# Second product of the quarter behind: two places of two slot tiles each instead of four places of one

## The reference, cut to what matters

```
h   = einsum('bsd,bdh->bsh', x, W[cat]) + b[cat]        # 4096 x 512
probs = softmax(h @ Wr);  eidx = argmax(probs)          # 8 experts
xe  = h[dispatch]                                       # per expert 512 slots x 512
hid = maximum(einsum('ecd,edf->ecf', xe, W1), 0)        # first product, F = 2048
ye  = einsum('ecf,efd->ecd', hid, W2)                   # second product
out = x + scatter_add(ye * p_tok)                       # rows back to their tokens
```

## Time and profile before

| | |
|---|---|
| runs | 805.10, 805.14, 805.49 us |
| profiled execution | 804.7 us, span 802.8 us |
| TensorE (matmul) | 791.8 us busy, 99% of the span |
| VectorE | 577.8 us, 72% |
| GpSimd | 511.1 us, 64% |
| ScalarE | 352.1 us, 44% |
| TensorE's granted clock | 1.000 |
| chain that ended last | 93% TensorE |

### The profile page before, as it was taken

How to read it: one execution, slowest core, us unless ns; L and a number is a source line. 1 busy time by engine, 2 the same in 40 slices (tenths; PEclk the granted TensorE clock), 3 DMA queues, 4 the chain that set the end, 5 groups by cost and what they waited for, 6 DMA issues and landing times.

```text
span 802.8 us, 14226 instructions
## 1 busy us (share of the span) xinstructions
PE 791.8 (99%) x5267; PEld 703.2 (88%) x5267; DVE 577.8 (72%) x760; ACT 352.1 (44%) x537; POOL 511.1 (64%) x392
## 2 busy tenths in 40 slices
PE   8999989999999999999999999999999999999997
PEld 5788869899999999999999999999999999999996
DVE  5677886788866896579657966787578866895532
ACT  4322336445444554445444644464445444554430
POOL 1000146866887688786887688768876888653601
PEclk9999999999999999999999999999999999999999
DMA  8987534631554355534444454425441544255201
GB/s 284 356 297 280 229 126 149 219 99 62 191 169 162 105 176 173 173 105 167 166 147 140 160 167 144 157 84 176 175 146 58 191 155 161 105 183 178 71 1 53
DMA packets 61103, 127.20 MB, mean 158 GB/s; under 512 B 8311, under 2 KB 8311, under 8 KB 60563
## 3 DMA queue, kind: packets, MB, share of 16 engines
q1 hardware_dynamic: 47714, 95.19, 34.0%
q0 software_dynamic: 13216, 31.38, 12.2%
q10 hardware_dynamic: 144, 0.26, 0.1%
HBM read 110.13 MB, written 25.17 MB: 169 GB/s over the span
## 4 chain that ended last, share of the span: by engine, by line
PE 93%; DVE 2%; DMA 2%; issue 1%; POOL 0%; SPq 0%; ACT 0%; POOLq 0%
PE y_ps L1505 44%; PE acc_ps L1408 20%; PE tp_ps L1408 19%; PE acc_ps L1314 5%; PE tp_ps L1314 2%; DMA stage<-x_t 1%; PE tp_ps L1240 1%; PE acc_ps L1422 1%; PE tp_ps L1422 1%; DMA early_rows<-h_rows,tok_all 1%; DVE xt_split L835 1%; PE y_ps L1220 0%; DVE rows L864 0%; DVE late_sel L932 0%; POOL early_rows L532 0%
## 5 line engine op out<-in xcount | busy, mean ns | idle before, releaser
L1505 PE MATMUL y_ps<-w_split,xt_split 128*128 128x512 f32 x1536 | 371.2, 391 | 0.5 <-issue 0.5
L1505 PEld LDWEIGHTS y_ps<-w_split,xt_split 128*128 128x128 f32 x1536 | 280.7, 188 | 53.9 <-issue 0.7
L1408 PE MATMUL acc_ps<-x_split,w_split 128*128 128x256 f32 x1320 | 180.8, 283 | 0.0
L1408 PE MATMUL tp_ps<-x_split,w_split 128*128 128x256 f32 x1284 | 176.4, 283 | 0.0
L1408 PEld LDWEIGHTS acc_ps<-x_split,w_split 128*128 128x128 f32 x1320 | 172.0, 191 | 4.7
L961 DVE TENSOR_TENSOR w_split<-stage,w_split 128x1024 fp32r<-128x1024 f32 x64 | 113.3, 1810 | 84.3 <-ACT w_split L670 84.3
L1408 PEld LDWEIGHTS tp_ps<-x_split,w_split 128*128 128x128 f32 x1284 | 167.6, 191 | 4.7
L546 POOL DMA_INDIRECT rows<-h_rows,idx_all x112 | 130.1, 1162 | 39.0 <-issue 32.3
L663 ACT ACTIVATE w_split<-stage 128x1024 fp32r<-128x1024 f32 x64 | 54.0, 843 | 92.8 <-PE acc_ps L1408 46.0
L503 POOL TENSOR_TENSOR w_sums<-stage 128x512 f32<-128x512 f32 x31 | 42.8, 1381 | 78.0 <-DVE w_split L950 69.2
L950 DVE TENSOR_TENSOR w_split<-stage,w_split 128x1024 fp32r<-128x1024 f32 x64 | 71.2, 1112 | 18.1 <-ACT w_split L663 18.1
(11 more groups left out here) (186 smaller groups left out, 803.5 us busy)
## 6 DMA issues: line engine op xcount, KB each, us to landing
stage<-w SPq DMA_DIRECT2D x64, 1024.0 KB, 6.3
b_rows<-x SPq DMA_DIRECT2D x8, 1024.0 KB, 9.4
h_rows<-rows POOLq DMA_DIRECT2D x6, 1024.0 KB, 9.8
stage<-cond_wt SPq DMA_DIRECT2D x4, 1024.0 KB, 9.5
x_more<-x_t SPq DMA_DIRECT2D x4, 1024.0 KB, 9.9
stage<-x_t SPq DMA_DIRECT2D x3, 1024.0 KB, 8.1
stage<-cond_w SPq DMA_DIRECT2D x3, 1024.0 KB, 9.5
h_rows<-rows SPq DMA_DIRECT2D x8, 256.0 KB, 2.6
```

The source lines that it names most:

```text
L1408: last = nc.tensor.matmul(out, w1s[wg][:, w, wb, k, f], xes[xg][:, a, xb, k, :], start=start and k == 0 and (w, a) == (HI, HI), stop=True, ...
L1505: last = nc.tensor.matmul(y_ps[:, s, :], hts[:, (q % 2) * QF + jj, a, s * P:(s + 1) * P], w2s[:, q % 2, w, jj, :], start=(first and jj == ...
```

## The change: what it does

In `step`, the second product's slot tile 1 moves from behind `second_and_sixth` to ahead of it, and slot tile 3 from behind `fourth` to ahead of it. No instruction is added or taken away, and no wait is changed; only TensorE's order is.

```diff
             def step(i, u):
                 first_and_fifth(i, u)
                 second_product(i, u - 1, 0)
+                second_product(i, u - 1, 1)
                 second_and_sixth(i, u)
-                second_product(i, u - 1, 1)
                 seventh_and_third(i, u)
                 second_product(i, u - 1, 2)
+                second_product(i, u - 1, 3)
                 fourth(i, u)
-                second_product(i, u - 1, 3)
```

## The result

| | before | after |
|---|---|---|
| median of the runs | 805.32 us (4 runs) | 815.99 us (4 runs, 815.43 to 816.37) |
| ratio | | 1.013 [1.0118, 1.0142] |
| span of the profiled execution | 802.8 us | 814.0 us |
| TensorE busy | 791.8 us | 794.1 us, 98% |
| first matmul of a second product to the last matmul's start | 652.85 us | 662.80 us |

The change makes the kernel 1.3% slower. Forecast were 814.2 us, 9.1 us more than before; the medians differ by 10.7 us. It grows by 9.95 us. It is the finest measure in this study, since it leaves out the first 145 us, in which the profiles of this study differ by up to 2.2 us (144.57 us in e7, 146.76 in e4).

A forecast was written before the change was run, and what follows sets the result against it. The loop's time was taken to be TensorE's matmuls, busy 589.12 of 589.12 us at full clock. Pace - 1.2, end + 1.6, step 4 + 8.7 and step 3 0 gave + 9.1: 805.14 becomes 814.2 us, range 805.5 to 819.

The forecast's parts named there:

- (a): TensorE's pace in the loop: 0.02 us gained per place entered, 59 places, 1.2 us gained.
- (b): `second_and_sixth` to `seventh_and_third`: cover falls from 2.75 us to none, 0.74 us are left; cost 0 in steps 2 and 5.
- (c): `fourth` to the next step: no loss in the loop; at the program's end a stall of 1.63 us, cost 1.6.
- (d): Step 3's `fourth` to step 4's P7a: VectorE's 13.79 us chain makes P7a wait 1.25 us, 7 times, 8.7 us.
- Rival 1: At step 4 splits and GpSimd's sums fall out of step, P7a never waits: 805.5 us; chance 0.13.
- (e): Step 2's `fourth` to step 3's P7a: the add ends in time, cost 0 by a margin of 0.4 us.
- rival 2: Step 3 stalls too, if GpSimd gets in first and holds up both W2 splits: + 4.5, 818.7 us; chance 0.17.
- The clock: TensorE's granted clock, 1.00 in the loop despite waits up to 1.3 us: nothing counted for it.

The follow-up runs named there:

- e7: Changed kernel with step 4's adds between the two W2 splits and tile 3 back behind `fourth` in the program's last step; 809.23 against 805.65 us before, 1.0046.
- e4: Changed kernel with GpSimd's four W1 sums waiting until VectorE's x and W2 splits of steps 3 and 4 are done; 806.24 against 805.32 us before, 1.0007.
- e1: Kernel before with only slot tile 1 moved, ahead of `second_and_sixth`; 805.03 against 805.32 us before, 0.9995.
- e5: Changed kernel with tile 3 back behind `fourth` in the program's last step alone; 814.39 against 805.65 us before, 1.0106.
- e6: Changed kernel with tile 3 back behind `fourth` in step 3 of every expert; 807.57 against 805.65 us before, 1.0023.
- e2: Kernel before with only slot tile 3 moved, ahead of `fourth`; 815.72 against 805.32 us before, 1.0129.
- e3: Changed kernel with both adds at step 4 between the two W2 splits; 806.41 against 805.32 us before, 1.0008.
- the pair of doses: `finish` of tile 0 ahead of step 4's adds, on the kernel before (805.41 against 805.38 us) and on the changed kernel (837.77 against 805.65 us).
- e9: Changed kernel with `finish` of tile 0 set ahead of the adds at step 4; 837.77 against 805.65 us before, 1.04.

## Why the prediction was right

- **(a), the pace:** 0.02 us for each place less, measured 0.021, in e1 (30 places, no other effect) and in the changed kernel (59). The trace of the changed kernel shows how it is made up: a run of 24 takes 5.47 us (457.94 to 463.41), two of 12 took 2 x 2.75.
- **(b), `second_and_sixth` right ahead of `seventh_and_third`:** 0.74 us of room forecast; e1 has 0.74 in the last expert's steps, from whose rows the forecast was made, and 0.81 in the loop, for the second add against P7b as for the first against P7a, and no wait. That this room was all there is left against a late ScalarE was not weighed; e6 and e7 paid for it. The changed kernel, with a copy late in six turns as well, kept 0.58 us of it: that it didn't pay was luck.
- **(c), the end:** 1.63 us forecast, 1.66 measured; e5 isolates it.
- **(d), step 4:** 1.25 us forecast, 1.28 measured, seven times; the chain was 13.79 us long in the forecast and 13.78 in the trace. e2, e3, e4 and the pair of doses show each link: the move, the chain on VectorE, GpSimd's part in it, and the lost cover. Rival 1, the chain that shrinks, needed the two engines out of step, and e4 shows that it would indeed have saved the waits; but both are released by the same split, so they move together. The size missed is the restart, 8 x 0.07 = 0.6 us.
- **(e), step 3:** 0 forecast, by a margin of 0.4 us; 0 measured, 0.74 us left. VectorE was first, as argued, so rival 2 did not happen.
- **The clock:** nothing counted, and nothing there in the loop. e9 shows how near that was: with one microsecond more per wait the clock alone would have cost 11.9 us.

The sum for the loop was +9.1 and came to +9.95: 0.6 the restarts, 0.24 the 0.03 us by which each wait is longer. The rest of the difference between 814.2 and 815.99 us lies ahead of the loop (0.7 us, with the dip of the clock in all four runs), and in the median of the kernel before, which was 0.2 us higher this time.

## What to carry to other kernels

When a group of instructions is moved behind another, ask what it releases: the whole chain that hangs on it moves too, so take its length from the trace and set it against the work that is left between the release and the wait. In a loop in which the bounding engine has no idle time, a reordering can gain only its pace (here 0.02 us a place) and can bring out every wait that the order of before had covered (here 1.35 us a turn). Cover that looks unused is an insurance: the hold-ups of 2.4 us in e6 and e7 would have fitted into it, though that was argued from the room of before and not run.

## What the runs showed of the hardware that was not expected

- Waits of 1.28 us, once in 85 us, left the granted clock at 1.00 (the changed kernel, seven times); waits of 2.32 us at the same place dropped it to the 1.2 GHz level for 3.4 us each time (e9). One microsecond more of waiting cost 1.04 us of its own and 1.7 of clock.
- Behind a wait TensorE needs 0.07 us to get back to its pace (195 ns from the first matmul to the second instead of 120).
- The pace gain sits at the entry into 512 columns: the first five matmuls of 512 columns behind ones of 256 follow each other at 233, 236, 228, 233 and 231 ns instead of 227; about 28 ns in all, of which 6 to 7 come back at the exit.
- ScalarE was held up for some 2.4 us and SyncE for about 1 at the loop's first step, in the same place in many turns of one build and in none of another that has the same code on ScalarE (e7 and e3). In the changed kernel the second copy at step 5, too, is 0.5 to 1.2 us late in the six turns that are followed by another, without a wait of TensorE behind it.
